# Two attention layers and two expert layers on one core: experts written out on GpSimd, key sums moved out of the first projections, second attention's sums copied out in two halves

## The reference, cut to what matters

```python
# layer 1: attention, 16 heads of 8
qkv = x @ W_attn + b_attn;  q, k, v = split(qkv)
s = q k^T;  s = s - mean(s);  mad = mean(|s|) + 1e-6
s = s / mad * gain;  masked to the causal half
r = max(s, 0) ** 4;  att = r / (sum(r) + 1e-6);  y = att v;  out = y @ W_proj + b_proj
# layer 2: 16 experts, each takes its 256 best tokens of 2048 (softmax gate), plus a shared expert
g, u = xg Wg^T, xg Wu^T;  h = gelu(g) * u;  eo = (h Wd^T) * weight
out = zeros.at[topk_idx].add(eo) + shared(x)
# layer 3: attention with a latent of 32, softmax(q k^T / sqrt(8)), causal
# layer 4: 8 experts, top 2 per token, silu(x W1) * (x W3) @ W2
```

## Time and profile before

| | us |
|---|---|
| median of 3 runs (lowest, highest) | 1144.07 (1141.48, 1144.14) |
| the profiled execution: its own time | 1145.06 |
| its span | 1143.3 |
| busy in the span: PE, DVE, ACT, POOL | 966.1, 750.8, 554.8, 352.7 |
| mean granted TensorE clock, share of full speed | 0.894 |

### The profile page before, as it was taken

One profiled execution on the slowest core, in us unless ns is written; L12 is line 12 of the kernel. 1 busy time (PEld: TensorE's weight loads), 2 busy tenths in 40 slices (PEclk: granted clock), 3 DMA queues, 4 the chain that ended last, 5 costly groups with the idle time before them and its releaser, 6 DMA issues.

```text
span 1143.3 us, 18275 instructions
## 1 busy us (share of the span) xinstructions
PE 966.1 (84%) x6011; PEld 474.3 (41%) x6011; DVE 750.8 (66%) x1543; ACT 554.8 (49%) x615; POOL 352.7 (31%) x785
## 2 busy tenths in 40 slices
PE   5699999999997764797817889999999888999996
PEld 3222223222324533686704333333333245566664
DVE  5879999999996585333334977777778116544446
ACT  2488889888985212221205024555555763222222
POOL 3053355335535000777632013333333430000000
PEclk8599999999998695899956559999999997999998
DMA  3401101110103011365433230222201100000001
GB/s 133 148 1 43 43 1 42 41 41 0 41 2 119 16 47 22 96 167 128 84 56 141 93 118 19 78 86 85 62 24 42 44 29 1 14 14 28 14 14 37
DMA packets 45655, 63.27 MB, mean 55 GB/s; under 512 B 7720, under 2 KB 33672, under 8 KB 42120
## 3 DMA queue, kind: packets, MB, share of 16 engines
q1 hardware_dynamic: 39968, 58.11, 16.3%
q0 software_dynamic: 5632, 4.46, 2.6%
HBM read 50.69 MB, written 11.86 MB: 55 GB/s over the span
## 4 chain that ended last, share of the span: by engine, by line
PE 55%; DVE 23%; issue 9%; ACT 4%; POOL 4%; DMA 4%; DVEq 0%; SPq 0%; POOLq 0%; ACTq 0%
PE causal_ps L1135 10%; PE acc_ps L748 8%; DVE mx L498 6%; PE acc_ps L1042 6%; PE tail_ps L988 5%; PE tail_ps L1145 5%; DVE R L1430 4%; PE causal_ps L1025 3%; DVE tails L1436 3%; PE causal_ps L710 2%; PE causal_ps L721 2%; DMA moe_rows<-out_e,idx_out 2%; ACT EX L1318 2%; POOL moe_rows L1989 2%; POOL G L1973 1%
## 5 line engine op out<-in xcount | busy, mean ns | idle before, releaser
L1318 ACT ACTIVATE EX<-causal_ps 128x1024 f32<-128x1024 f32 (+1 forms) x160 | 146.9, 939 | 156.0 <-PE causal_ps L1025 154.4
L498 DVE TENSOR_REDUCE mx<-tail_ps 128x1 f32<-128x512 f32 x266 | 157.4, 633 | 39.7 <-PE tail_ps L991 21.4
L1205 ACT ACTIVATE R<-R 128x2048 f32<-128x2048 f32 (+1 forms) x80 | 134.7, 1737 | 0.5 <-DVE R L1430 0.5
L1135 PE MATMUL causal_ps<-XT,w 128*128 128x512 f32 x256 | 117.3, 606 | 2.6 <-DVE hid_f L1808 1.9
L988 PE MATMUL tail_ps<-KM,QM 72*128 72x512 bf16 (+1 forms) x320 | 104.5, 355 | 8.8 <-DVE mx L498 3.0
L1025 PE MATMUL causal_ps<-QE,KE 75*128 75x512 bf16 (+3 forms) x384 | 102.2, 337 | 8.5 <-ACT EX L1318 3.1
L1354 ACT ACTIVATE act_f<-causal_ps 128x512 f32<-128x512 f32 x64 | 38.2, 597 | 130.0 <-PE causal_ps L1135 130.0
L1212 ACT ACTIVATE R<-R 128x1792 f32<-128x1792 f32 (+4 forms) x80 | 100.4, 1268 | 0.0
L1430 DVE TENSOR_SCALAR R<-causal_ps 128x1024 f32<-128x1024 f32 (+1 forms) x88 | 93.9, 1070 | 9.7 <-PE causal_ps L710 8.6
L1436 DVE TENSOR_REDUCE tails<-causal_ps 128x1 f32<-128x768 f32 (+4 forms) x96 | 92.8, 967 | 10.6 <-PE causal_ps L721 9.9
L2049 POOL TENSOR_TENSOR pacer<-eps_ln 128x1 f32<-128x1 f32 x160 | 31.2, 195 | 206.9 <-ACT EX L1318 206.2
(11 more groups left out here) (266 smaller groups left out, 1615.0 us busy)
## 6 DMA issues: line engine op xcount, KB each, us to landing
QS<-q_parts SPq DMA_DIRECT2D x8, 576.0 KB
KS<-k_parts SPq DMA_DIRECT2D x24, 192.0 KB
QM<-q_parts SPq DMA_DIRECT2D x8, 576.0 KB
KM<-k_parts SPq DMA_DIRECT2D x24, 192.0 KB
QE<-q_parts SPq DMA_DIRECT2D x8, 576.0 KB
KE<-k_parts SPq DMA_DIRECT2D x24, 192.0 KB
wg<-in_wg_t SPq DMA_DIRECT2D x16, 256.0 KB
wu<-in_wu_t SPq DMA_DIRECT2D x16, 256.0 KB
```

Source lines behind the costliest of these rows:

```text
L498: return reduce(mx[:, par, hh, o0:o0 + step * (cnt - 1) + 1:step], scores[:, 0:cnt * w].rearrange("p (c w) -> p c w", w=w), AX.X, op, **how)
L1135: mm = pe.matmul(banks[2 * ring + o], w[:, k, m * P:(m + 1) * P], XT[:, n * BANK:(n + 1) * BANK], start=True, stop=True)
L1205: act.activation(R4[:, rp, h0:h0 + 2, 0:width], R1[:, rp, h0:h0 + 2, 0:width], ACT.Square).then_inc(squared, 1)
L1318: act.activation(EX[:, rp, hh, 0:width], causal_ps[hh % 2][:, 0:width], ACT.Exp, scale=float(D) ** -0.5).then_inc(exp_done, 1)
```

## The change

1. Experts on GpSimd are written out, with no loop. The indices are read from `idx` directly, `idx_in`, `idx_out` and `carry_waits` go. `out_e` has four slots, so `weigh` waits for the scatter four before. The gather of expert e+5 stands ahead of scatter e.
2. Prologue: `proj` lies in half of R4, and the first rests write into the other half, so q stays whole. The sums over later keys are made on GpSimd in a chain of one-column instructions (a copy and six additions), behind DVE's `k_tiles`, which now follows Y. PE's product with `k_heads` is out of the batch loop and stands ahead of the first fill. DVE copies `corr` at the first job of step 1 of quad 0. GpSimd's bias addition to X stands behind its quad 0.
3. Second attention: ACT copies half 0 of acc_ps (columns 0 to 511, whole once step 3's sums are in) between the exps of heads 2 and 3 of the last step, and half 1 where it copied all before.

```diff
-        proj = R1[:, :, :, :].rearrange("p a h t -> p (a h t)").rearrange("p (m t) -> p m t", t=T)
+        proj, rests0 = R4[:, 1, :, :], R4[:, 0, :, :]
...
-                    pe.wait_ge(corr_ready, b + 1)
-                    for i in range(KT - 1):
-                        mm = pe.matmul(acc_ps[:, b * BANK + i * H:b * BANK + (i + 1) * H],
-                                       proj[:, 2 * b, i * P:(i + 1) * P], k_heads[:, b, i, :], start=True, stop=True)
-                    mm.then_inc(corr_full, 1)
+            for b in range(B):
+                pe.wait_ge(corr_ready, b + 1)
...
+                mm.then_inc(corr_full, 1)
...
-                            at_least(pe, e_out, g)
                             pe.wait_ge(v_ready, NQ + g + 1)
+                    if s == 0:
+                        at_least(pe, e_out, 2 * g - 1 + k)
...
-                pe.wait_ge(e_out, g + 1)
+                pe.wait_ge(e_out, 2 * (g + 1))
...
             act.wait_ge(part_done, 2 * REP * B)
+            act.wait_ge(corr_full, B)
...
-            def exp_evacuate(g):
-                act.wait_ge(exp_summed, NS * (g + 1))
-                at_least(act, e_turned, g)
-                act.activation(Esb[:, :], acc_ps[:, :], ACT.Copy).then_inc(e_out, 1)
+            def exp_evacuate(g, half):
+                act.wait_ge(exp_summed, NS * (g + 1) - 1 + half)
+                if half == 0:
+                    at_least(act, e_turned, g)
+                cols = slice(half * BANK, (half + 1) * BANK)
+                act.activation(Esb[:, cols], acc_ps[:, cols], ACT.Copy).then_inc(e_out, 1)
...
                         if (s, hh) == (0, 1) and not first:
-                            exp_evacuate(g - 1)
+                            exp_evacuate(g - 1, 1)
+                        if (s, hh) == (NS - 1, 2):
+                            exp_evacuate(g, 0)
...
-                link(dve.tensor_reduce(k_tiles[:, b, :], k.rearrange("p (i t) -> p i t", t=P), AX.X, ALU.add))
-                dve.wait_ge(upto_ready, 6)
-                link(dve.tensor_tensor(k_later[:, :, :], later[:, :, :],
-                                       k_tiles[:, b, :].unsqueeze(1).broadcast_to([P, KT - 1, KT]), ALU.mult))
-                link(dve.tensor_reduce(k_after[:, :], k_later[:, :, :], AX.X, ALU.add))
...
-                dve.wait_ge(corr_full, b + 1)
-                take_rests(0, b, proj)
+                take_rests(0, b, rests0, proj)
...
+                dve.tensor_reduce(k_tiles[:, b, :], k.rearrange("p (i t) -> p i t", t=P), AX.X, ALU.add
+                                  ).then_inc(key_sums, 1)
+            def take_corr():
+                dve.wait_ge(corr_full, B)
...
+                    if j == STEP_AT[1] and first:
+                        take_corr()
...
-                if k >= 2 or not isinstance(j, int) or j > 0:
-                    dve.wait_ge(scattered, 16 * NH * (4 * j + k - 1))
+                if not isinstance(j, int) or j > 0:
+                    dve.wait_ge(scattered, 16 * NH * (4 * j + k - 3))
...
+            def sum_later_keys(b):
+
+                pool.wait_ge(key_sums, b + 1)
+                pool.tensor_copy(k_after[:, b, KT - 2:KT - 1], k_tiles[:, b, KT - 1:KT]).then_inc(key_step, 1)
+                for i in range(KT - 3, -1, -1):
+                    pool.wait_ge(key_step, (KT - 1) * b + KT - 2 - i)
+                    pool.tensor_tensor(k_after[:, b, i:i + 1], k_after[:, b, i + 1:i + 2], k_tiles[:, b, i + 1:i + 2], ALU.add
+                                       ).then_inc(key_step, 1)
+                pool.wait_ge(key_step, (KT - 1) * (b + 1))
+                pool.tensor_tensor(k_heads[:, b, :, :], k_after[:, b, :].unsqueeze(2).broadcast_to([P, KT - 1, H]),
+                                   own_head[:, :].unsqueeze(1).broadcast_to([P, KT - 1, H]), ALU.mult
+                                   ).then_inc(corr_ready, 1)
+
+            pool.wait_ge(upto_ready, 4)
+            sum_later_keys(0)
+            pool.wait_ge(v_sb, 1)
+            take_v(0, 0)
+            sum_later_keys(1)
+            pool.wait_ge(v_sb, B)
+            quad(0, 0, after=0)
             pool.wait_ge(x_in, 16)
             pool.wait_ge(w_in, 16 * 2)
             pool.tensor_tensor(X[:, :, :], X[:, :, :], YT[:, 0, 0:P].unsqueeze(1).broadcast_to([P, NT, P]),
                                ALU.add).then_inc(res_in, 1)
...
+            def gather(e):
+                if e >= 4:
+                    pool.wait_ge(g_sb, e - 3)
                 for h in range(NH):
...
+            def scatter(e):
                 pool.wait_ge(out_sb, e + 1)
+                if e:
                     pool.wait_ge(scattered, 16 * NH * e)
-                carry_waits()
                 for h in range(NH):
+                    pool.indirect_dma_start(out=moe_rows, in_=out_e[:, e % 4, h, :], in_offset=None,
+                                            out_offset=bass.IndirectOffsetOnAxis(ap=idx[:, e, h:h + 1].bitcast(U32), axis=0),
                                             compute_op=ALU.add).then_inc(scattered, 16)
...
+            for e in range(4):
+                gather(e)
             pool.wait_ge(sh_out, 16 * CH)
+            gather(4)
+            for e in range(E0):
+                if e + 5 < E0:
+                    gather(e + 5)
+                scatter(e)
```

More of the change, by code:

```diff
@@ L237, in build @@
         k_tiles = sb("k_tiles", [P, B, KT], F32, A)
-        later = sb("later", [P, KT - 1, KT], F32, A)
-        k_later = sb("k_later", [P, KT - 1, KT], F32, A)
-        k_after = sb("k_after", [P, KT - 1], F32, A)
+        k_after = sb("k_after", [P, B, KT - 1], F32, A)
         own_head = sb("own_head", [P, H], F32, A)
@@ L687, in _ @@
                     mm.then_inc(v_full, 1)
-                    pe.wait_ge(corr_ready, b + 1)
-                    for i in range(KT - 1):
-                        mm = pe.matmul(acc_ps[:, b * BANK + i * H:b * BANK + (i + 1) * H],
-                                       proj[:, 2 * b, i * P:(i + 1) * P], k_heads[:, b, i, :], start=True, stop=True)
-                    mm.then_inc(corr_full, 1)
+            for b in range(B):
+                pe.wait_ge(corr_ready, b + 1)
+                for i in range(KT - 1):
+                    mm = pe.matmul(acc_ps[:, b * BANK + i * H:b * BANK + (i + 1) * H],
+                                   proj[:, 2 * b, i * P:(i + 1) * P], k_heads[:, b, i, :], start=True, stop=True)
+                mm.then_inc(corr_full, 1)
             pe.wait_ge(w_in, 16 * 2)
@@ L1391, in take_rests @@
                         dve.wait_ge(part_done, 2 * REP * (B * layer + b) + 2 * n + m + 1)
-                        dve.tensor_tensor(rest, values[m][:, :] if values and n == 0 else rest, pt[:, m, n, :],
+                        src = (values[m][:, :] if layer else values[:, 2 * b + m, :]) if n == 0 else rest
+                        dve.tensor_tensor(rest, src, pt[:, m, n, :],
                                           ALU.subtract).then_inc(rest_done, 1)
@@ L1960, in _ @@
             pool.nop().then_inc(masks_ready, 1)
-            def carry_waits():
-                pool.tensor_tensor(carrier[:, :], eps_ln[:, :], eps_ln[:, :], ALU.add)
-            def gather(e, k):
-                src = idx[:, e, :] if isinstance(e, int) else idx[:, bass.ds(e, 1), :].rearrange("p o h -> p (o h)")
-                pool.tensor_copy(idx_in[:, k, :], src).then_inc(idx_ready, 1)
-            def fetch(k):
-                for h in range(NH):
-                    pool.indirect_dma_start(out=G[:, k, h, :], out_offset=None, in_=xs_rows,
-                                            in_offset=bass.IndirectOffsetOnAxis(ap=idx_in[:, k, h:h + 1].bitcast(U32), axis=0)
-                                            ).then_inc(gathered[k], 16)
@@ L1983, in scatter @@
+            def scatter(e):
                 pool.wait_ge(out_sb, e + 1)
-                if not (isinstance(e, int) and e == 0):
+                if e:
                     pool.wait_ge(scattered, 16 * NH * e)
-                carry_waits()
                 for h in range(NH):
-                    pool.indirect_dma_start(out=moe_rows, in_=out_e[:, k % 2, h, :], in_offset=None,
-                                            out_offset=bass.IndirectOffsetOnAxis(ap=idx_out[:, k, h:h + 1].bitcast(U32), axis=0),
+                    pool.indirect_dma_start(out=moe_rows, in_=out_e[:, e % 4, h, :], in_offset=None,
+                                            out_offset=bass.IndirectOffsetOnAxis(ap=idx[:, e, h:h + 1].bitcast(U32), axis=0),
@@ L1991, in scatter @@
                                             compute_op=ALU.add).then_inc(scattered, 16)
-            ORDER = [("g", 0), ("g", 1), ("s", 0), ("g", 2), ("s", 1), ("g", 3), ("s", 2), ("s", 3)]
-            def scat_at(j, k):
-                order = ORDER if not isinstance(j, int) or j < 3 else [o for o in ORDER if o[0] == "s"]
-                return order.index(("s", k)) + 1
             pool.wait_ge(idx_sb, 1)
             pool.wait_ge(xs_out, 16 * 2)
```

(26 more changed lines are left out.)

53 lines of the change are left out of this document (19 added, 34 removed).

## The result

The changed kernel took 1129.91 us (median of 4 runs, 1128.91 to 1132.92), the kernel before 1144.11 us beside it on the same chip (1141.48 to 1151.11). The ratio is 0.9871 (0.9876 by these two medians alone), with a 95% interval of 0.9823 to 0.9918: faster by 14.2 us. The forecast was 1130.1. The profiled execution has a span of 1127.9 us against 1143.3, 15.4 less; the forecast by its own sum was 14.0 less.

The account below looks back on a forecast made before the run. It took PE with DVE behind as the main bound, and the order of scatters among the experts. Terms -12.5 - 4.8 + 3.3 = -14.0 against 1145.06 gave 1131.1, or 1130.1 us by the median; range 1120 to 1139.

Parts of the forecast that it names:

- Prologue: Start of the kernel: first fill at 37.4 instead of 42.65, 5.2 less; net 4.8 us less after the corr copies.
- The 0.45 for the copies of corr: First attention: DVE's corr copies move into a stretch where DVE ends last and cost all of their 0.45 us.
- The case that the prologue gives nothing: Rival, prologue: at 0.9 us per GpSimd step the fill starts where it did; 1135.3 us in all, chance 0.11.
- Moving the addition on X: First attention: GpSimd's 4.50 us on X, now behind quad 0, is hidden and costs 0; uncovered, 4.5 once.
- Experts: Expert stage: scatters every 6.75 us with a gather ahead, 5.5 without; 12.5 us less, bounds 16.9 and 1.0 less.
- up to 0.48 behind it: Experts: the gap between carrier and issue, up to 0.48 us, was counted among what goes.
- the four copies ahead of the first gather: Start of the experts: four index copies ahead of the first fetch go, 0.55 us.
- Second attention: Second attention's halves: each turn 0.25 us later at 7 boundaries (1.8), the end 1.5; together 3.3 us more.
- Halves win: Rival, second attention: exp of head 3 has slack, each turn comes 0.43 sooner; 3.4 less, 1123.4 us, chance 0.17.
- Landing takes over: Rival, experts: landing is 5.6 us each time, period stays 7.8, only 1.0 less; 1141.6 us, chance 0.10.
- Each boundary pays the whole 3.06: Rival, second attention: held exp passes its whole 3.06 us delay to each boundary, 22.9 more; 1149.7 us, chance 0.07.

Follow-up runs that it names:

- e1: Kernel before with only the prologue part of the change; 1138.43 us, ratio to the kernel before 0.9944.
- e4: Changed kernel with half 0 copied behind the exp of head 3 instead of ahead of it; 1121.69 us, ratio to the kernel before 0.9791.
- e7: Changed kernel with two slots of out_e instead of four; 1130.95 us, ratio to the kernel before 0.9872.
- e9: Changed kernel with GpSimd's addition to X put back ahead of the key sums; 1135.82 us, ratio to the kernel before 0.9920.
- e10: Changed kernel with a one-column GpSimd instruction again ahead of each scatter's two transfers; 1132.16 us, ratio to the kernel before 0.9891.
- e8: Changed kernel with weight loads from the fifth expert on cut to two columns, computing with the first four's weights; 1125.63 us in one run.
- e3: Kernel before with only the experts written out on GpSimd; 1135.13 us, ratio to the kernel before 0.9917.
- e2: Kernel before with only the second attention's copy in two halves; 1148.07 us, ratio to the kernel before 1.0020.
- e5: Changed kernel with PE's product for batch 1 moved behind the first six fills of quad 0; 1126.10 us, ratio to the kernel before 0.9822.

## Why the prediction was right

The forecast was 14.0 less and the span came 15.4 less, and in part this is luck. Of the 15.4 some 2.2 are no effect of the change (1.2 ahead of the first den, where only one boundary was changed, and 1.0 of the 1.5 ahead of the experts). The rest gave 13.2, the experts less than forecast and the prologue more, and each part came to its number by other terms than those forecast, as follows.

**Prologue** (4.8 forecast). The fill came 5.86 earlier instead of 5.2. XT was in 0.6 us sooner in this execution (in the chain of waits its transfer takes 3.94 us against 4.54), but this did not carry over, because PE's first eight products took longer. The timelines of the changed kernel and of the kernel before, in this order:

```profile
5.35 6.41 PE L673 MATMUL causal_ps<-XT,w_attn 128*128 128x512 f32 x8 [5.35 <-DMA XT<-in_xT]
5.96 5.31 PE L677 MATMUL causal_ps<-XT,w_attn 128*128 128x512 f32 x8 [5.96 <-DMA XT<-in_xT]
```

So k was ready at 13.32 + 0.75 = 14.07, 0.5 later than the 13.57 of the forecast. What won was the rest of the path: from there to the end of the second k_tiles (30.21 + 1.21 = 31.42) it is 17.35 where the forecast had 18.03; from there to PE's product 2.36 against 2.6, as GpSimd's chain with the spread takes 2.25 and was put at 2.3 + 0.3; and from the product's start to the fill 3.01 against 3.2. The 0.45 for the copies of corr does not show. The first attention is 0.42 longer here, but with the same copies it took 316.44 us in e1, 316.54 in e4 and 316.62 in e7, against 316.45 before. In the changed kernel's execution PE's clock also rose a little later (granted clock 0.69 from 54 to 56 us, 0.83 in e4, 0.85 in e7, 1.00 in e1). The case that the prologue gives nothing is out by e1.

**Moving the addition on X** was costed at nothing by the earlier trace rows. That holds: e1 has the addition in its new place, and its first attention takes as long as before (316.44 against 316.45). e9 shows what it would cost ahead: 4.3 us of the rests, of which 3.1 reached the fill. The rule of the Trainium skill (SBUF — State Buffer, Who interferes with whom), that a DVE instruction with two SBUF inputs contends with a GpSimd instruction that reads SBUF, agrees: 9.04 against 4.78.

**Experts** (12.5 forecast). A period with a gather ahead was 6.80 on average, forecast 6.75; it came as a mix of 6.43 and 7.1 to 8.0, as said. There are ten of them, not eleven as I had counted, and the five without a gather took 5.86 instead of 5.5: I took 0.45 from landing to the next issue, and it is 0.73 (549.28 to 550.01), the term of this part that was mis-sized. Fifteen periods make 97.3 us, forecast 96.25 (11 x 6.75 + 4 x 5.5). The forecast counted the carrier and up to 0.48 behind it as won. With the carrier alone put back, e10 has 0.16 behind it where no landing is waited for and 0.40 to 0.49 where one is, and a period by issue of 6.48. So the carrier of a scatter is worth 0.05 to 0.07 a period, and the 0.48 that stood in the kernel before without a wait for a landing (carrier at 523.07, issue at 523.74) did not belong to it; to what it belonged is open. The slots are out by e7. What is left is the index copies with their joints, the carriers ahead of the gathers, the loop, and the order: before, two scatters stood together once in four experts, and GpSimd waited 1.55 to 1.95 us between them (1.95 ahead of the carrier at 529.41), where a gather stands now. None of these was put back alone, so their shares are not shown.

The stage gave 10.3 where that step's share of 12.5, less the 0.55 of the four copies ahead of the first gather, is 12.0. Of the missing 1.7, 1.1 is in these periods, and 0.6 is that the first scatter is issued 20.13 behind the first gather, where the forecast had 475.9 - 456.4 = 19.5. The forecast also read the chain of the kernel before wrongly: it is not transfers and GpSimd from 476 us on. Up to 498.62 PE's products hold it, and GpSimd takes it over only at 502.54.

The rule of the Trainium skill (DMA: Bandwidth & Descriptors, SWDGE vs HWDGE vs iDMA) speaks of turns that each transfer engine takes between GpSimd's queue and the hardware queues. e8 agrees with it and gives a size: without the loads three of the four long periods go and the stage is 2.4 us shorter.

**The stage ahead of the experts** gave 1.5, of which 0.55 was forecast. The other 1.0 is no part of the change: PE's clock stood at 0.67 instead of 0.50 from 430 to 440 us, and with the same code there e4 and e7 gave 0.6 to 0.7 and e3 1.8. e2, which has nothing of the change up to there, gave 0.8.

**Second attention** (3.3 lost, 2.97 measured between the dens). The sum is right and its terms are not. Between the dens lie six of the seven boundaries, which by the forecast cost 1.5, and the end. The six cost 0.6 (2.97 less 2.37), the first 0.15 (4.58 us from step 3's last sums to the turn against 4.43), and the one shown 0.06, not 0.25: half 0 starts 0.92 behind the start of step 3's last sums and not 0.98, and I put the held exp 0.60 behind it, but it starts 0.49 behind (728.77 to 729.26). By these two the sums of step 4 come 2.71 behind step 3's and not 2.88, and the turn 4.57 and not 4.76; 0.19 less at six boundaries is 1.1 us. The end costs 2.37, not 1.5: 1.49 is the two waits of PE, as forecast and as e2 and e7 show, and 0.88 is the turn at 1.2 GHz. The errors cancel, and the second of them is chance: with a turn at 2.4 GHz the loss between the dens would have been 2.1, as it was 2.0 in e2. That the exp of head 3 holds back the sums is shown by e4, which moves nothing else.

**The other cases.** Halves win: out by e2, and shown under which order they would, by e4. Landing takes over: it does in four periods of ten, for about 2.4 us in all. Each boundary pays the whole 3.06: out, as six of them together pay 0.6.

## What to carry to other kernels

When a copy is cut in halves so that one may leave early, ask which instruction the early half stands ahead of on its in-order engine, and put it behind what the consumer of the other half needs: the same two instructions lost 2.0 to 3.0 us in one place and won 3.3 in the next. Where a chain of transfers sets the period, count the issues and joints of the engine that issues them, and take the time from landing to next issue from a row; a small instruction in front of it can be nearly free (here 0.05 to 0.07 us a period). An independent product ahead of the first big stage is worth moving behind it, but it will be paid in part where it lands.

## What was not expected of the hardware

- PE's clock rose from 1.2 to 2.4 GHz at about 60 us before, 55 after, 68 in e3 and 66 in e9, and e3 has the very same instructions as before up to there. Where it rose about 8 us later behind the first fill, the first attention was 3.0 us (e3) and 3.5 us (e9) longer than before, about as much as the smallest effect looked for here. Parts under 3 us are to be read from stages, not from spans.
- With the same two waits of 1.72 and 0.81 us ahead of it, the last turn took 1.94 us in the changed kernel and in e10, and 1.06 in e2, e5, e7, e8 and e9.
- A GpSimd instruction of 0.20 us between two issues lengthened the period by 0.05 only (6.48 against 6.43).
